# Experts' rests: a small expert's unit and a large expert's unit done in one step

## The reference, cut to what matters

```python
shared_out = _swiglu(xf @ shared_gate_up.T) @ shared_down.T
affinity = sigmoid(xf @ gate_w.T)
_, sel = top_k(affinity + expert_bias, 3)
sel_aff = take_along_axis(affinity, sel, axis=1)
gating = sel_aff / (sel_aff.sum(axis=-1, keepdims=True) + 1e-09)
combined = einsum('td,efd->tef', xf, expert_gate_up)     # 2 * D_FF columns for each expert
hidden = _swiglu(combined)                               # silu(gate) * up
expert_out = einsum('tef,edf->ted', hidden, expert_down)
routed_out = einsum('tk,tkd->td', gating, take_along_axis(expert_out, sel[:, :, None], axis=1))
x = x + shared_out + routed_out
```

## Time and profile before

| what | value |
|---|---|
| runs shown | 1440.11, 1439.57, 1436.03 us, median 1439.57 |
| span of the profiled execution | 1442.9 us |
| expert loops in it | 604.41 to 1040.24 us |
| TensorE busy | 1308.7 us, 91% of the span |
| ScalarE, VectorE, GpSimd busy | 467.2, 583.3, 200.8 us |
| DMA | 97.06 MB, mean 67 GB/s |

### The profile page before, as it was taken

How to read it: one execution, slowest core, us unless ns; L and a number is a source line. 1 busy time by engine, 2 the same in 40 slices (tenths; PEclk the granted TensorE clock), 3 DMA queues, 4 the chain that set the end, 5 groups by cost and what they waited for, 6 DMA issues and landing times.

```text
span 1442.9 us, 18224 instructions
## 1 busy us (share of the span) xinstructions
PE 1308.7 (91%) x5770; PEld 831.9 (58%) x5771; DVE 583.3 (40%) x1559; ACT 467.2 (32%) x1004; POOL 200.8 (14%) x207
## 2 busy tenths in 40 slices
PE   4899999999999899899898998988669999999798
PEld 3554485566466454377565775665445567565365
DVE  9999732111243351111111111111175333685894
ACT  5899632122122200011111111111113233227884
POOL 1000000000000055010100111101263000022370
PEclk8999999999999899999999999999879989999899
DMA  9100000000101214231246115253462000100001
GB/s 223 55 1 1 2 1 1 1 1 1 77 31 32 95 50 129 97 126 49 94 150 216 44 44 195 66 199 95 164 177 100 1 30 1 67 0 1 1 23 51
DMA packets 40976, 97.06 MB, mean 67 GB/s; under 512 B 4205, under 2 KB 6567, under 8 KB 39745
## 3 DMA queue, kind: packets, MB, share of 16 engines
q1 hardware_dynamic: 27205, 68.70, 14.3%
q0 software_dynamic: 6240, 16.39, 4.2%
q10 hardware_dynamic: 7452, 10.97, 2.1%
HBM read 79.91 MB, written 16.10 MB: 67 GB/s over the span
## 4 chain that ended last, share of the span: by engine, by line
PE 75%; DVE 11%; DMA 4%; issue 3%; ACT 3%; ACTq 1%; DVEq 1%; another core or an unknown queue 1%; POOL 0%; POOLq 0%
PE psum L433 38%; PE psum L1813 13%; PE psum L1868 7%; PE psum L1793 4%; DMA slot_outs<-sb_blk 3%; PE psum L2008 3%; PE psum L461 2%; DVE sb_hT_conv L1408 1%; PE psum L1951 1%; PE psum L1893 1%; PE psum L1925 1%; ACT sb_htok L807 1%; DMA sb_blk<-rows,sb_blk 1%; PE psum L1843 1%; DVE sb_blk L1201 1%
## 5 line engine op out<-in xcount | busy, mean ns | idle before, releaser
L433 PE MATMUL psum<-sb_w_reg,sb_blk 128*128 128x256 f32 x896 | 207.3, 385 | 1.2 <-issue 1.2
L433 PEld LDWEIGHTS psum<-sb_w_reg,sb_blk 128*128 128x128 f32 x896 | 170.1, 193 | 33.7 <-issue 12.4
L1813 PE MATMUL psum<-sb_z_reg_r,sb_hT_conv_r 125*125 125x512 f32 x400 | 170.9, 427 | 0.2 <-issue 0.2
L433 PE MATMUL psum<-sb_w_reg,sb_hT_conv 128*125 128x512 f32 (+1 forms) x376 | 168.6, 598 | 0.0
L1813 PE MATMUL psum<-sb_htok_r,sb_hT_conv_r 125*125 125x512 f32 x300 | 118.8, 396 | 0.0
L433 PE MATMUL psum<-sb_hT_conv,sb_w_reg 128*128 128x416 f32 (+3 forms) x336 | 108.2, 481 | 8.1 <-ACT sb_hT_conv L467 8.1
L1198 DVE TENSOR_TENSOR sb_blk<-sb_blk,psum 128x256 f32<-128x256 f32 x56 | 23.6, 421 | 227.4 <-ACT sb_blk L781 227.4
L433 PEld LDWEIGHTS psum<-sb_w_reg,sb_hT_conv 128*125 128x125 f32 (+1 forms) x376 | 68.6, 188 | 76.9 <-issue 76.3
L1868 PE MATMUL psum<-sb_w_reg,sb_blk 128*128 128x512 f32 x224 | 109.2, 610 | 2.2
L760 ACT CAST sb_hT_conv_r<-sb_a_reg 125x625 fp32r<-125x625 f32 x80 | 56.1, 715 | 116.6 <-PE psum L1813 116.5
L433 PEld LDWEIGHTS psum<-sb_hT_conv,sb_w_reg 128*128 128x128 f32 x336 | 67.2, 204 | 44.4 <-issue 40.3
(11 more groups left out here) (388 smaller groups left out, 1815.7 us busy)
## 6 DMA issues: line engine op xcount, KB each, us to landing
sb_hT_conv<-w_expert SPq DMA_DIRECT2D x7, 2048.0 KB, 12.5
sb_w_reg<-w_expert SPq DMA_DIRECT2D x6, 2048.0 KB, 10.6
sb_hT_conv<-w_expert SPq DMA_DIRECT2D x7, 1024.0 KB
slot_outs<-sb_blk ACTq DMA_DIRECT2D x28, 256.0 KB
sb_w_reg<-w_expert SPq DMA_DIRECT2D x6, 1024.0 KB, 12.6
sb_w_reg<-w_gnn SPq DMA_DIRECT2D x1, 4096.0 KB, 43.8
sb_w_reg<-w_qkv SPq DMA_DIRECT2D x1, 3072.0 KB, 20.5
slot_outs<-sb_blk ACTq DMA_DIRECT2D x1, 2560.0 KB, 10.5
```

Source lines behind the costliest of these rows:

```text
L433: ins = e.matmul(out, l, r, start=(n == 0), stop=(n == len(pairs) - 1))
L1813: ins = e.matmul(psum[0:TP, b, :], counts_at(l, 2 * i + n // NT)[:, s % HALF_T, :], z[s], start=(n == 0), stop=(n == len(pairs) - 1))
```

## The change

A **step** takes the place of a unit. A step does one unit of a small expert and one unit of a large expert: the small expert of turn t and the rest of the large expert of turn t - 1, whose weights still lie in their slot. Turn t is now: steps, `slot_free`, whole blocks. The number of steps is the larger of the two counts of units, and at least one; where one of the two has no unit left, a dummy is done (in turn 0 there is no large expert yet). One gather brings 64 rows, 32 of each. TensorE does gate and up of both, then for each in turn the transposition of the hidden values and the product with down, into two banks. ScalarE does two silu, one copy of both results, and two writes. Each step reads its own table word with the two unit numbers. A block's write is split into two DMAs of 64 rows, so that `s_out` counts 32 for blocks and steps alike. SyncE loads a turn's small and large expert together, small first, once the steps of the turn before have ended (turn 0: once the shared expert's up products have). The table is computed anew. Three small VectorE instructions with their waits ahead of it, which gave every large expert at least one unit of rest, go.

```diff
         def counts_of(e, turn):
-            word = from_table(e, T_COUNTS, turn, 0, (PER_BLOCK + 1) << A_REST)
...
+        def step_units(e, turn, i):
+
+            word = from_table(e, T_STEPS, turn + i * N_TURNS, 0, (DUMMY_A + 1) << UNIT_A_AT)
+            return (within(e, word & ((1 << UNIT_A_AT) - 1), 0, DUMMY),
+                    within(e, word >> UNIT_A_AT, 1, DUMMY_A))
...
             with e.Fori(0, pairs) as pair:
                 for j in range(2):
-                    for kind, slot in ((T_A, a_slots[j]), (T_B, LAST_SLOT)):
-                        x = number_of(e, kind, pair * 2 + j)
-                        free = 2 * j + (2 if kind == T_B else 1)
-                        e.wait_ge(slot_free, pair * 4 + free)
-                        sync_weights(e, x, slot)
+                    turn = pair * 2 + j
+                    number_b, number_a = number_of(e, T_B, turn), number_of(e, T_A, turn)
+                    free = from_table(e, T_NEED, turn, 2, N_TURNS + 3)
+                    e.wait_ge(slot_free, free)
+                    sync_weights(e, number_b, LAST_SLOT)
+                    sync_weights(e, number_a, a_slots[j])
...
+        def pool_steps(e, steps, g, turn):
+
+            with e.Fori(0, steps) as i:
+                unit_b, unit_a = step_units(e, turn, i)
                 e.wait_ge(s_xt, g + i + 1)
-                pool_gather(e, g + i, unit + i, UNIT)
+                e.tensor_copy(idx[0:UNIT], idx_all[0:UNIT, bass.ds(unit_of(e, unit_b), 1)]).then_inc(s_col, 1)
+                e.tensor_copy(idx[UNIT:2 * UNIT], idx_all[UNIT:2 * UNIT, bass.ds(unit_of(e, unit_a - 1), 1)]).then_inc(s_col, 1)
+                pool_rows(e, g + i, 2 * UNIT)
...
-            e.wait_ge(s_out, g * 16 + 16)
+            e.wait_ge(s_out, g * 32 + 32)
             e.copy(y_blk, psum[:, 5, :]).then_inc(s_y, 1)
             e.wait_ge(s_y, g + 2)
-            e.dma_start(outs_dram[bass.ds(unit_of(e, unit) * UNIT, SLOTS), :], y_blk).then_inc(s_out, 16)
+            slots = outs_dram[bass.ds(unit_of(e, unit) * UNIT, SLOTS), :]
+            for n in range(2):
+                e.dma_start(slots[n * 64:(n + 1) * 64, :], y_blk[n * 64:(n + 1) * 64]).then_inc(s_out, 16)
+
+        def act_step(e, g, turn, i):
+
+            units = step_units(e, turn, i)
+            for n in range(2):
+                e.wait_ge(s_gu, g * 2 + n + 1)
+                e.activation(silg[:, n, 0:128], psum[:, 1 + n, 0:128], ACT.Silu).then_inc(s_sil, 1)
             act_copy_rows(e, g + 1)
             e.wait_ge(s_dn, g + 1)
-            e.wait_ge(s_out, g * 16 + 16)
-            e.copy(y_blk[:, 0:128], psum[:, 5, 0:128]).then_inc(s_y, 1)
+            e.wait_ge(s_out, g * 32 + 32)
+            e.copy(y_blk[:, 0:256].rearrange("p (u n) -> p u n", u=2), psum[:, 5:7, 0:128]).then_inc(s_y, 1)
             e.wait_ge(s_y, g + 2)
-            e.dma_start(outs_dram[bass.ds(unit_of(e, unit) * UNIT, UNIT), :].rearrange("t (c n) -> c t n", c=KD),
-                        y_blk[:, 0:128]).then_inc(s_out, 16)
+            for n, unit in enumerate(units):
+                e.dma_start(outs_dram[bass.ds(unit_of(e, unit) * UNIT, UNIT), :].rearrange("t (c n) -> c t n", c=KD),
+                            y_blk[:, n * 128:(n + 1) * 128]).then_inc(s_out, 16)
...
+        def pe_step(e, slot_a, landing, g):
+
+            b, a_ = expert_views(LAST_SLOT), expert_views(slot_a)
+            e.wait_ge(ld_up[LAST_SLOT], landing)
             e.wait_ge(s_xe, g + 1)
             e.wait_ge(s_hid, g * 2 + 2)
+            for n, (w_gu, _) in enumerate((b, a_)):
+                for k in range(KD):
+                    both = w_gu[:, k, :].rearrange("p (u n) -> p u n", u=2)
+                    for c in range(PER_BLOCK):
+                        ins = e.matmul(psum[c * UNIT:(c + 1) * UNIT, 1 + n, 0:256].rearrange("p (u n) -> p u n", u=2),
+                                       xgT[:, k, n * UNIT:(n + 1) * UNIT], both[:, :, c * 128:(c + 1) * 128],
+                                       start=(k == 0), stop=(k == KD - 1))
+                ins.then_inc(s_gu, 1)
+            e.wait_ge(ld_down[LAST_SLOT], landing)
+            e.wait_ge(s_y, g + 1)
             e.wait_ge(s_he, g * 2 + 2)
+            for n, (_, w_dn) in enumerate((b, a_)):
+                e.wait_ge(s_hid, g * 2 + n + 3)
+                e.transpose(psum[:, 3 + n, 0:128], hid[:, n * 128:(n + 1) * 128], ident).then_inc(s_ht, 1)
+                if n == 0:
+                    pe_turn_rows(e, g + 1)
+                e.wait_ge(s_he, g * 2 + n + 3)
+                for k in range(KD):
+                    for c in range(PER_BLOCK):
+                        ins = e.matmul(psum[c * UNIT:(c + 1) * UNIT, 5 + n, 0:128], hidT[:, n, k * UNIT:(k + 1) * UNIT],
+                                       w_dn[:, k, c * 128:(c + 1) * 128], start=(k == 0), stop=(k == KD - 1))
             ins.then_inc(s_dn, 1)
...
-                    pe_rest(e, rest_b, LAST_SLOT, turn * 16 + 16, g)
+                    g, steps, whole = counts_of(e, turn)
+                    pe_steps(e, steps, a_slots[1 - j], turn * 16 + 16, g)
                     pe_slot_free(e)
-                    g = g + rest_b
+                    g = g + steps
                     with e.Fori(0, whole) as i:
                         pe_block(e, a_slots[j], pair * 16 + 16, g + i)
-                    pe_rest(e, rest_a, a_slots[j], pair * 16 + 16, g + whole)
-                    pe_slot_free(e)
```

More of the change, by code:

```diff
@@ L51 @@
 DUMMY = MAX_UNITS
+DUMMY_A = DUMMY + PER_BLOCK
+MOST_STEPS = PER_BLOCK - 1
 UNITS = MAX_UNITS + 2 * PER_BLOCK
@@ L598, in sync @@
                 x = number_of(e, T_B, turn)
-                free = from_table(e, T_NEED, turn, 4, 3 * N_TURNS)
+                free = from_table(e, T_NEED, turn, 2, N_TURNS + 3)
                 e.wait_ge(slot_free, free)
@@ L640, in pool_gather, with pool_rows @@
         def pool_gather(e, g, unit, rows):
-            e.tensor_copy(idx, idx_all[:, bass.ds(unit_of(e, unit), 1)]).then_inc(s_col, 1)
-            e.wait_ge(s_col, g + 1)
+            e.tensor_copy(idx, idx_all[:, bass.ds(unit_of(e, unit), 1)]).then_inc(s_col, 2)
+            pool_rows(e, g, rows)
+        def pool_rows(e, g, rows):
+            e.wait_ge(s_col, g * 2 + 2)
             e.sem_inc(s_pass, 1)
@@ L702, in gpsimd @@
             with e.Fori(0, turns) as turn:
-                g, rest_b, whole, rest_a = counts_of(e, turn)
-                unit, unit_b = units_of(e, turn)
-                pool_rest(e, rest_b, g, unit_b)
-                g = g + rest_b
+                g, steps, whole = counts_of(e, turn)
+                unit = first_unit(e, turn)
+                pool_steps(e, steps, g, turn)
+                g = g + steps
                 with e.Fori(0, whole) as i:
@@ L709, in gpsimd @@
                     pool_gather(e, g + i, unit + i * PER_BLOCK, SLOTS)
-                pool_rest(e, rest_a, g + whole, unit + whole * PER_BLOCK)
             with e.Fori(turns, end) as turn:
-                g, rest_b, _, _ = counts_of(e, turn)
-                pool_rest(e, rest_b, g, units_of(e, turn)[1])
+                g, steps, _ = counts_of(e, turn)
+                pool_steps(e, steps, g, turn)
             total = block_at(e, end)
@@ L1895, in pe_unit, with pe_steps @@
             ins.then_inc(s_dn, 1)
-        def pe_rest(e, rest, slot, landing, g):
-            with e.Fori(0, rest) as i:
-                pe_unit(e, slot, landing, g + i)
+        def pe_steps(e, steps, slot_a, landing, g):
+            with e.Fori(0, steps) as i:
+                pe_step(e, slot_a, landing, g + i)
         def pe_slot_free(e):
-            e.matmul(psum[0:1, 6, 0:2], ident[:, 0:1], ident[:, 0:2], start=True, stop=True).then_inc(slot_free, 1)
+            e.matmul(psum[0:1, 7, 0:2], ident[:, 0:1], ident[:, 0:2], start=True, stop=True).then_inc(slot_free, 1)
```

170 lines of the change are left out of this document (78 added, 92 removed).

## The result

| what | before | changed |
|---|---|---|
| median of the runs beside each other | 1437.8 us (4 runs) | 1414.88 us (4 runs, 1411.04 to 1417.98) |
| ratio, 95% interval | | 0.9847, 0.9820 to 0.9874 |
| span of the profiled execution | 1442.9 us | 1409.3 us |
| first step or unit to the last write's landing | 435.83 us | 410.70 us |

Of the 33.6 us between the two spans, 25.1 lie in the expert loops, 4.2 ahead of them and 4.3 behind, where the change edits nothing but the table. Over all profiles of this case the loops begin at 599.6 to 605.7 us (602.54 in a second profile of the kernel before), and what follows the last write's landing takes 392.4 to 402.9 us (402.7 and 402.1 before; 398.4, 399.0 and 392.6 changed).

The account below looks back on a forecast made before the run. TensorE bounds block stretches, a chain through all engines the changes. Savings 10.7 + 4.7 + 1.7 + 1.4 + 6.4 = 24.9 us take 1442.9 to 1418.0; less 3.3 for the median, 1415 us. Range 1404 to 1434, the forecast's own 1408 to 1423.

Parts of the forecast that it names:

- A change: Between large experts, with one step: 9.9 us each, first silu at 5.2 us; four take 39.6 for 50.3, 10.7 us saved.
- The fifth change, the first and the last step: Two-step change 17.8 us, first step 7.8, last step's landing 14.1 to 14.3; saving 4.7, 1.7 and 1.4 us.
- The block stretches: Whole blocks of turns 1 to 5: excess over 11.59 us a block falls from 13.1 to 6.7, 6.4 us saved.
- a change has one copy where it had two: ScalarE in a change: the small unit's copy no longer waits for a just-issued write, removing turn 4's 2.6 us and its like.
- The stall behind a step: First block's copy waits for the step's writes under load, stalling TensorE in the second block: 0.8 us, six times.
- d + 19.3: Landing of a step's writes 19.3 us after d, the begin of its last product; claimed stall 4.2 us.
- rival 3: Step's writes land only with both weight loads' end: stall 4.2 and clock 1.9 us, six times; 1445 us, slower; chance 0.06.
- At no cost: Extra idx copy, table words, later loads and each block's second DMA (0.55 us, in ScalarE's 3.36 us idle time) are hidden.
- Rival 1: A step is as long as two units: changes stay 12 us, a following step 9.5; 1429 us; chance 0.15.
- Rival 4: Block stretches without stall or clock fall: 13.1 us saved instead of 6.4, a change of 9.5; about 1406 us; chance 0.08.
- Rival 2: Second write starts only behind the first: stall 3.1 and clock fall 1.9 us each time; 1438 us, no change; chance 0.11.

Follow-up runs that it names:

- b2: Kernel before, units kept, with only SyncE's load order changed: small and large expert loaded together behind the small unit, small first; 1412.64 us, ratio 0.988.
- a1: Changed kernel with query, key and value weights laid out in DRAM so their load moves 2 KB rows; 1407.3 us, ratio 0.9848.
- c5: Changed kernel with ScalarE's first-unit word read behind the steps and query, key and value weights in 2 KB rows; 1401.06 us, ratio 0.982.
- d1: Changed kernel with each block's write whole, ScalarE's first-unit word behind the steps, and query, key and value weights in 2 KB rows; 1398.35 us, ratio 0.9745.
- a4: Changed kernel with ScalarE's table word for the blocks' first unit read behind the steps, not ahead; 1408.15 us, ratio 0.9837.

## Why the prediction came out right, point by point

**Right, in the sum.** 24.9 us were forecast from the first unit to the landing of the last write, 25.1 came off in the profiled execution; the median fell by 22.9 to 1414.88, forecast 1415. That it met the number so closely is in part luck, of two kinds. The other two comparisons gave 16.8 and 12.3 us, and the means of the profiles 20.4 over the same stretch. And two errors in the sum, below, nearly cancel.

**A change.** Forecast 9.9 us and the first silu 5.2 us after the last product; measured 9.41 to 9.48 where the clock held, and 5.04. Every step of that chain came out within 0.5 us. Four changes: 38.8 us for a forecast of 39.6, though one has a clock fall.

**The fifth change, the first and the last step.** 17.8, 7.8 and 14.3 us forecast, 17.7, 7.4 and 13.8 measured. But the first step gains by the loads alone: b2 takes 5.1 us there, and the step with its dummy costs 2.3 against that.

**The block stretches: wrong cause, and the size by luck.** 6.4 us were forecast off; 4.6 came off in the first pair of profiles, 1.1 by the means (excess 10.9 before, 9.8 changed). The step of the prediction that failed is "a change has one copy where it had two". b2 keeps both copies and takes the excess to 2.0: what held the copy was that the large expert's weights were loaded between the two units. In the first pair the term should have stood as 11 us for the order of the loads, and a loss of 6.5 for what the step and the split write bring back; by the means, 9 and 8.

**The stall behind a step.** I charged 0.8 us for each of six. Five cost 0.2 in the mean, by their excess (the write lands 14.6 us after the last product begins, 723.1 less 708.50, not 16 to 17), the sixth cost 7.3. There the landing is at d + 19.3 (984.63 less 965.31), the very figure of rival 3, and the loss exceeds its 6.1 us. But the figure is met by chance. Rival 3 has the write land with the end of both loads, and the load of w_qkv landed at 988.1 (issued at 967.87, 20.2 us), 3.5 us behind the write; in a1, with the same bytes, the write landed 9 us ahead of it. What holds it is the size of the rows, in the one turn where the second load is not an expert's. I had read the packets of the earlier trace rows as if every load had them. (By the prediction's own formula a landing at d + 19.3 stalls by 4.0 us, not 4.2.) Whether the write is slow because it runs on four engines, as the prediction says, no run tests.

**"At no cost": wrong for the split write.** Between blocks it is hidden: in both kernels the silu behind a block's copy waits 2.79 us for TensorE, and the pair takes 1.14 us of them. In a change I charged its 0.55 us. What I did not see is what comes with 0.55 us on the path: clock falls, in 7 of 16 changes against none of 8 with the write whole, and a double issue at the one place where the copy is late. With the write whole the stretches up to turn 5's end take 386.9 and 390.0 us, with it split 399.9 in the mean.

**What the gain is made of**, by the means of the profiles: 419.3 us before; 403.4 with the loads moved (16 off); 388.5 with the steps and the write whole (15 off); 399.9 as changed (11 given back). For the loads I had credited 8.1 (6.4 and 1.7), for the split charged 2 to 3 us within the changes. The prediction's sum for these stretches, 23.5, met 23.2 in the first pair of profiles and 19.4 in the means: two large errors nearly cancel, and part of the rest is how often the clock falls.

**Rivals.** Rival 1 (a step as long as two units) is refuted by changes of 9.4 us. Rival 4 (no stall, no fall) is what the changed kernel would be without turn 5 and the split: c5 and d1, whose ratios 0.982 and 0.9745 lie about its 0.977, show that. Rival 2 (landing at d + 18.4, a fall each time) is refuted by the same row of turn 1, d + 14.6, and by stalls of 0.2 us. Rival 3's loss is there in one turn only, and by another mechanism.

## What to carry to other kernels

Before a rearrangement of work is credited with a gain, make alone the one edit in it that costs nothing, here the place at which the loads start; and keep a large load away from a small write that others wait for, or give the load small rows. An instruction that is hidden 28 times is not hidden the few times its engine is late: look for the stretch where the cover is gone.

## What the runs showed of the hardware

- **The row size of a foreign load sets how long a small write takes.** The second of two writes of 64 KB (264 packets together) lands 11.6 to 12.2 us after issue beside a load in 2 KB packets, 13.9 to 16.5 us (seven profiles) beside one whose packets are 3.5 KB in the mean, 2 KB and 24 KB mixed. Without a load it takes 2.4 to 2.5 us.
- **Issuing two DMAs on ScalarE can take twice its usual time**: a block's pair usually takes 1.14 us, and 1.20 beside a load at 2 KB packets. For the late block of turn 5 it took 2.27 to 2.76 beside the tail of the load with large rows, where one DMA took 0.39. The load isn't the whole reason: the last block's pair took 1.3 to 1.9 us though the load had landed (in the changed kernel the load at 988.1, the pair from 998.18 on in 1.49 us). What holds it stays open.
- **SyncE is held at its fourth load in a row**, 6.65 to 8.46 us in the changed kernel. By SyncE's order of time:

```profile
710.40 0.44 SPq L566 DMA_DIRECT2D sb_hT_conv<-w_expert  x1
711.02 0.60 SPq L565 DMA_DIRECT2D sb_w_reg<-w_expert  x1
711.81 7.22 SPq L566 DMA_DIRECT2D sb_w_reg<-w_expert  x1
```

- **Clock falls came and went with half a microsecond.** With 2.5 us of TensorE idle ahead of the transposition three changes of four had one, with 2.0 us 7 of 16 (always the third change, never the first two), with 1.5 us or less none of 20.
- **The releaser that a profile names can have ended long before.** "3.55 <-PE" in a4 stood for 2.4 us of ScalarE's own sequencer; only the versions in which that got shorter showed it.
